# State space: B and C projected once and convolved along time by ACT and VectorE, with z and the first x tap moved forward on TensorE

## The chip, the cores and the metric

One Trainium2 chip, one NeuronCore. The metric is the device time of one execution in microseconds (us); lower is better.

## The reference

The program is a two-layer decoder over 16 sequences of 128 rows and 256 columns: in layer 0 linear attention, cross attention and a gated MLP with ternary weights, in layer 1 a state-space block, attention with 8-bit inputs and a ternary linear layer, each followed by a residual sum and a layer norm. The change touches the state-space block alone:

```python
zxbcdt = x @ W_in.T                       # z 512, xBC 768 (x 512, B 128, C 128), dt 64
z, xBC, dt_raw = ...
y = conv_general_dilated(xBC, w, padding=[(3, 0)], feature_group_count=768)   # 4 taps along time, each channel by itself
xBC = y * sigmoid(y)
dt = softplus(dt_raw + dt_bias);  a = dt * -exp(A_log)
CB = C @ B.T                              # 128 x 128 for one sequence
y = (CB * L * dt) @ x + D * x             # L[i, j] = exp(sum of a over j+1..i), lower triangle
out = rmsnorm(y * silu(z)) @ W_out.T
```

## The kernel before

All data stay in SBUF in 32-bit floats. One sequence is one tile of 128 rows. The state-space stage (`state_space`, line 1160) is a software pipeline of 18 steps m = 0 to 17, written out for each engine by `steps(m, side, attend, front, back, first)`. In step m the part called front works on sequence m + 1 (projections, convolution, softplus, decays), attend on sequence m (the seven levels of the masked product), and back on sequence m - 1 (gate, output projection, norm). Each engine runs its own fixed list, and semaphores tie the lists together. Step 0 also holds the last pieces (`tail`) of the MLP of layer 0, and steps 1 to 14 prepare the 8-bit weights of the next stage in 12 chunks: `chunk_mean` (L1585, L1587, VectorE) and `centre` (L1357, POOL) in steps 1 to 10, `chunk_high` (L1508, ACT) in steps 2 to 13, `chunk_low` (L1602, VectorE) in steps 3 to 14. GpSimd is called POOL here.

TensorE in step m, in order: dt (L1444, 2 products); B and C into the PSUM bank pC (L1451): for each half, 4 taps times 2 halves of the contraction, 16 products, whose weights are the projection's columns already multiplied by the tap's coefficient (`w_tap`), and whose moving operand is the transposed input xT shifted by the tap; levels 0 and 1 (L1404); the transposes of the gated y (L1424), which wait for VectorE's gate; z (L1462); then the eight x taps (L1410) with, before tap n = 0, 2, 4, 5, 6, levels 2 to 6; before tap 2 the product CB (L1472), which waits for `bc_in`; with tap 4 the output projection (L1433). At the end the transposes of the next input (L1392) and the seven decay sums (L1489). A product of 32-bit operands shows in the trace as two matmul records (the transposes as one).

A level waits for the VectorE product of the level two before it: `pe.wait_ge(s_term_done, level l - 2)`, since only two PSUM banks (pL) hold levels. So level 4 waits for term 2.

VectorE in step m: dt plus bias (L1296), minus |dt| (L1298), gate y (L1625), terms 0 and 1 (L1618), start of y (L1631), softplus (L1561, L1563, L1565, L1570, L1572, L1575, L1577) and a (L1580), `chunk_low`, term 2, `chunk_mean`, term 3, the masked CB (L1650, L1652), norm (L112), terms 4 and 5, residual and statistics (L1664, L98 to L103), term 6, xdt (L1671), and the scaled inputs xd of levels 0 to 3 (L1248).

ACT: exp of minus |dt| (L1524), gated y out of PSUM and its squares (L1515, L1517), Ln with its table load (L1530), Silu of B and C into bcT with its table load (L1532), Silu of z (L1534), `chunk_high`, Silu of x (L1544), the copy of the transposed input (L1286), Exp of the decays with its table load (L1548).

POOL: for each of the seven levels y += term (L1350), each waiting for its term; the root (L1338, L1340) after level 1; `centre` after levels 3 and 4; the norm's root (L107); skip (L1370); the scaled inputs of levels 4 to 6 (L1248).

The weights `w_tap` are made by `make_tap` (L1274) on VectorE in the last steps of the stage before.

Of the kernel before, what the change touches and what calls it, by code (L numbers as in the profile page):

```python
# [22 lines left out]
ACT = mybir.ActivationFunctionType  # L23
# [3 lines left out]
P = 128  # L27
# [1132 lines left out]
def state_space(nc, env, dram, ctx, spare):  # L1160
# [18 lines left out]

    w_z, w_dt, w_raw, conv_w, w_out, norm_w, dt_bias, a_neg, d_skip, spans, pairs = [env.ssm[n] for n in (  # L1180
        "z", "dt", "bcx", "conv", "out", "norm", "dt_bias", "a_log", "d", "spans", "pairs")]
    sz = sb("sz", [P, 2, HID])
# [4 lines left out]
    bcT = sb("bcT", [P, 2 * N])  # L1187
    w_tap = env.w_tap = sb("w_tap", [P, TAPS, KT, CONV])
    xT = sb("xT", [P, KT, PAD + P])
    dt_in = sb("dt_in", [P, H])  # L1190
# [23 lines left out]
             "xdt_done", "xd_vector", "cbd_done", "skip_done", "y0_done", "gated", "squared",  # L1214
             "ms_eps", "rms_done", "yT_ps", "yT_in", "o_ps")
    s = {n: sem(n, 1) for n in names}
# [55 lines left out]
    def make_tap(dve, tap):  # L1272

        last = dve.tensor_tensor(w_tap[:, tap], w_raw[:], conv_w[:, tap, :].unsqueeze(1).to_broadcast([P, KT, CONV]),  # L1274
                                 ALU.mult)
        if tap == TAPS - 1:
            last.then_inc(taps_ready, 1)
            dve.wait_ge(a_exp, 1)
            dve.tensor_scalar(a_neg[:], a_neg[:], -1.0, None, ALU.mult).then_inc(w_ready, 1)
# [107 lines left out]
    def tensor(pe, tail):  # L1387
# [7 lines left out]
        def steps(m, side, attend, front, back, first):  # L1395
# [41 lines left out]
            if front:  # L1437
                pe.wait_ge(s["xT_in"], now(m + 1, 0))
                if m > 1:
                    pe.wait_ge(norm.summed, now(m - 2, 0))  # L1440
                else:
                    pe.wait_ge(s["dec_in"], now(m, 0))
                for k in range(KT):
                    last = pe.matmul(dt_bank(m + 1), xT[:, k, PAD:PAD + P], w_dt[:, k, :],  # L1444
                                     start=(k == 0), stop=(k == KT - 1))
                last.then_inc(s["dt_ps"], 1)
                pe.wait_ge(s["cbd_done"], now(m, 0))
                for half in range(2):
                    for n in range(TAPS * KT):
                        t, k = n // KT, n % KT  # L1450
                        last = pe.matmul(pC[:, half * N:(half + 1) * N],  # L1451
                                         w_tap[:, t, k, HID + half * N:HID + (half + 1) * N],
                                         xT[:, k, t:t + P],
                                         start=(n == 0), stop=(n == TAPS * KT - 1))
                last.then_inc(s["bc_ps"], 1)
            next_level()
            next_level()
            if back:
                transpose_gated(m - 1)
            if front:  # L1460
                for k in range(KT):
# [6 lines left out]
                pe.wait_ge(s["xs_in"], now(m, 0))  # L1468
            for n in range(TAPS * KT):
                if n == 2 and front:  # L1470
                    pe.wait_ge(s["bc_in"], now(m + 1, 0))
                    pe.matmul(pC[:, 0:P], bcT[:, 0:N], bcT[:, N:2 * N], start=True, stop=True)\  # L1472
                        .then_inc(s["cb_ps"], 1)
                if n in (0, 2, 4, 5, 6):
                    next_level()
# [22 lines left out]
    def scalar(act, tail):  # L1498
# [13 lines left out]
        def steps(m, side, attend, front, back, first):  # L1512
# [7 lines left out]
            if back and not front:  # L1520
                gated_out(m - 1)
            if front:
                act.wait_ge(s["minus_abs"], now(m + 1, 0))
                act.activation(e_abs[:], e_abs[:], ACT.Exp).then_inc(s["e_done"], 1)  # L1524
# [5 lines left out]
                act.activation(log_p[:], one_p[:], ACT.Ln).then_inc(s["log_done"], 1)  # L1530
                act.wait_ge(s["bc_ps"], now(m + 1, 0))
                act.activation(bcT[:], pC[:, 0:2 * N], ACT.Silu).then_inc(s["bc_in"], 1)  # L1532
                act.wait_ge(s["z_ps"], now(m + 1, 0))
# [21 lines left out]

    def vector(dve, tail):
        def softplus(m):


            dve.wait_ge(s["e_done"], now(m, 0))  # L1560
            dve.tensor_scalar(one_p[:], e_abs[:], 1.0, None, ALU.add).then_inc(s["one_p_done"], 1)  # L1561
            dve.wait_ge(s["one_p_done"], now(m, 0))
            dve.tensor_scalar(part[:], one_p[:], -1.0, 1e-30, ALU.add, ALU.max).then_inc(s["part_min"], 1)  # L1563
            dve.wait_ge(s["part_min"], now(m, 0))
            dve.reciprocal(part[:], part[:]).then_inc(s["part_inv"], 1)  # L1565
# [689 lines left out]
def program(nc, dram, out):  # L2255
    env = Env()
    with ExitStack() as ctx:
# [31 lines left out]
        def regions(at, shapes):  # L2289
            tiles = {}  # L2290
            for n, shape in shapes:
# [5 lines left out]
                              ("out", [4, D]), ("norm", [4]), ("dt_bias", [64]), ("a_log", [64]), ("d", [64]),  # L2297
                              ("spans", [7, P]), ("pairs", [7, P])))
        with ExitStack() as xa:
# [86 lines left out]
def layouts(i):  # L2386
# [16 lines left out]
    a["ssm_win"] = t("L1_attn_W_in")  # L2403
    a["ssm_conv"] = np.broadcast_to(t("L1_attn_conv_w"), (P, 4, 768))
    a["ssm_wout"] = t("L1_attn_W_out")
    a["ssm_norm"] = np.asarray(i["L1_attn_norm_w"]).reshape(-1, P).T
# [36 lines left out]
```

## Time and profile before

| | |
|---|---|
| median of 3 runs | 2179.44 us (2178.09 to 2184.95) |
| profiled execution | 2178.37 us, span 2176.6 us |
| PE busy | 2028.2 us, 93% |
| VectorE busy | 1624.8 us, 75% |
| ACT busy | 1333.5 us, 61% |
| POOL busy | 1274.6 us, 59% |
| state-space stage | about 860 to 1274 us of the span |

The span is the profiled execution from its first to its last instruction, 1.8 us shorter than that execution's device time. Shares are means over six stages with different limits. PE is TensorE's matmuls, PEld its weight loads.

### The profile page before, as it was taken

The numbers are of one execution on the slowest core, as the hardware profiler recorded it, in microseconds if no ns is written. First come the engines' busy times: TensorE is split into PE (matmuls) and PEld (weight loads), VectorE is DVE, ScalarE is ACT, GpSimd is POOL, SyncE is SP. The second block draws the span as 40 slices with busy tenths as digits, with TensorE's granted clock in tenths as the row PEclk, the third lists the DMA queues.
The fourth block names the chain that finished last, engine by engine and source line by source line (L and its number), as shares of the span: only waits on it lengthen the run. The fifth ranks groups of instructions, "written<-read, shape, count | busy, mean of one in ns | idle before, by whom it ended". The sixth has DMA issues, their size and how long they took to land.

```text
span 2176.6 us, 35701 instructions
## 1 busy us (share of the span) xinstructions
PE 2028.2 (93%) x10116; PEld 1329.1 (61%) x10116; DVE 1624.8 (75%) x3833; ACT 1333.5 (61%) x5022; POOL 1274.6 (59%) x1550
## 2 busy tenths in 40 slices
PE   7879999999999998899999957999999999999995
PEld 5636666666666665555655524666666666666664
DVE  7845667677776777787888746788888888788886
ACT  3555666666666665333343326777777777777773
POOL 0154454455444542578876734777777777777774
PEclk9999999999999999999999979999999999999998
DMA  6000000000000003000000011000000000000000
GB/s 225 1 18 6 3 4 3 2 5 2 2 2 2 2 1 141 9 20 20 20 20 10 1 47 40 4 4 6 6 6 5 6 5 6 8 5 6 3 3 8
DMA packets 30094, 37.62 MB, mean 17 GB/s; under 512 B 3328, under 2 KB 24320, under 8 KB 29312
## 3 DMA queue, kind: packets, MB, share of 16 engines
q1 hardware_dynamic: 29952, 36.11, 5.0%
q8 instruction: 42, 0.69, 0.1%
q14 instruction: 100, 0.82, 0.1%
HBM read 34.00 MB, written 2.10 MB: 17 GB/s over the span
## 4 chain that ended last, share of the span: by engine, by line
PE 63%; DVE 15%; ACT 11%; issue 7%; POOL 3%; DMA 0%; DVEq 0%; SPq 0%; POOLq 0%; ACTq 0%
PE xa_pS L755 5%; PE xa_pJB L736 5%; PE xa_pO L830 5%; PE xa_pY L867 5%; PE fa_pJB L1910 5%; PE xa_pJA L736 4%; PE ssm_pX L1410 4%; PE fa_pS L1929 3%; PE fa_pY L1962 3%; PE fa_pO L1949 3%; PE fa_pJA L1890 2%; PE ssm_pL L1404 2%; PE fa_pH L2012 2%; PE xa_pP L747 2%; POOL fa_rs L1846 2%
## 5 line engine op out<-in xcount | busy, mean ns | idle before, releaser
L2038 ACT ACTIVATE fa_qT<-fa_pH,all_fa_head_vec 128x512 f32<-128x512 f32 x128 | 99.6, 778 | 177.9 <-PE fa_pH L2012 177.9
L1846 POOL TENSOR_TENSOR fa_rs<-fa_rs,all_minus_half 128x4 f32<-128x4 f32 x192 | 197.9, 1031 | 15.0
L1350 POOL TENSOR_TENSOR ssm_y<-ssm_y,ssm_term 128x512 f32<-128x512 f32 x112 | 142.2, 1270 | 81.5 <-DVE ssm_term L1618 57.1
L2047 ACT ACTIVATE fa_pS<-fa_pS,fa_nb 128x128 f32<-128x128 f32 x512 | 183.3, 394 | 6.0 <-issue 6.0
L1843 POOL TENSOR_TENSOR fa_rs<-fa_ms,all_eps5w 128x4 f32<-128x4 f32 x192 | 44.4, 232 | 226.8 <-ACT fa_q_junk L2031 126.4
L1929 PEld LDWEIGHTS fa_pS<-fa_kT,fa_qT 128*128 128x128 f32 x1024 | 124.1, 191 | 65.2 <-ACT fa_qT L2038 58.4
L1871 POOL TENSOR_TENSOR fa_cat<-fa_ov,fa_om 128x512 bf16<-128x512 f32 x128 | 154.0, 1203 | 5.3
L1929 PE MATMUL fa_pS<-fa_kT,fa_qT 128*128 128x128 f32 x1024 | 148.1, 288 | 2.6 <-ACT fa_qT L2038 0.9
L1862 POOL TENSOR_TENSOR fa_ov<-fa_ob,fa_om 128x512 f32<-128x512 bf16 x128 | 148.0, 1157 | 3.2 <-DVE fa_om L2225 3.2
L682 POOL TENSOR_TENSOR xa_rs<-xa_ms,all_eps 128x4 f32<-128x4 f32 (+1 forms) x65 | 13.2, 203 | 222.6 <-ACT xa_junk L906 222.6
L924 ACT ACTIVATE xa_pr<-xa_pS,xa_nb,xa_rs 128x256 f32<-128x256 f32 x256 | 142.5, 568 | 0.2
L2180 DVE TENSOR_TENSOR fa_qn<-fa_pJA,fa_rs 128x512 f32<-128x512 f32 x128 | 88.4, 690 | 69.0 <-POOL fa_rs L1846 68.9
L1962 PE MATMUL fa_pY<-all_shared_weights,fa_cat 128*128 128x256 bf16 x1024 | 133.6, 274 | 4.8 <-POOL fa_cat L1871 4.8
L2031 ACT ACTIVATE fa_q_junk<-fa_pJA 128x128 bf16<-128x128 f32 x512 | 136.4, 302 | 0.4
L2047 ACT ACTIVATION_READ_ACCUMULATOR fa_pS<-fa_pS,fa_nb 128x1 f32 x512 | 134.0, 262 | 0.0
L1890 PE MATMUL fa_pJA<-fa_w_all,fa_xq 128*128 128x512 bf16 x512 | 133.0, 383 | 0.0
L1949 PE MATMUL fa_pO<-fa_pT,fa_v 128*128 128x256 f32 x512 | 131.9, 380 | 1.1 <-DVE fa_ob L2208 1.0
L1910 PE MATMUL fa_pJB<-all_shared_weights,fa_ctxT 128*128 128x512 f32 x256 | 126.2, 617 | 5.6 <-DMA fa_ctxT<-in_ctxT 4.9
L755 PE MATMUL xa_pS<-all_shared_weights,xa_qT 128*128 128x256 f32 x512 | 126.4, 387 | 5.3 <-ACT xa_qT L931 5.2
L1410 PE MATMUL ssm_pX<-ssm_w_tap,ssm_xT 128*128 128x512 f32 x256 | 122.6, 592 | 0.0
L867 PE MATMUL xa_pY<-xa_wo,xa_oT 128*128 128x256 f32 x512 | 121.4, 380 | 1.0 <-ACT xa_oT L952 1.0
L736 PE MATMUL xa_pJA<-all_shared_weights,xa_xT 128*128 128x512 f32 x256 | 121.5, 597 | 0.4 <-DVE xa_t L987 0.2
(330 smaller groups left out, 5844.7 us busy)
## 6 DMA issues: line engine op xcount, KB each, us to landing
all_shared_weights<-in_fa_w SPq DMA_DIRECT2D x12, 512.0 KB, 3.8
fa_cat<-in_fa_wproj SPq DMA_DIRECT2D x8, 512.0 KB, 3.8
all_shared_weights<-in_xa_wq SPq DMA_DIRECT2D x1, 2048.0 KB, 13.8
xa_wo<-in_xa_wo SPq DMA_DIRECT2D x1, 2048.0 KB, 17.2
xa_ctxT<-in_ctxT SPq DMA_DIRECT2D x16, 128.0 KB, 2.1
all_shared_weights<-in_fa_wkvx SPq DMA_DIRECT2D x1, 2048.0 KB, 10.0
fa_ctxT<-in_ctxT SPq DMA_DIRECT2D x16, 128.0 KB, 2.1
out_x<-all_X SPq DMA_DIRECT2D x16, 128.0 KB, 1.7
```

Of the source, the lines that this page charges most:

```text
L736: last = pe.matmul(bank[:, :], lhs[k], w[:, k, at0:at0 + 512], start=(k == 0), stop=(k == KT - 1))
L755: last = pe.matmul(pS[b][:, (h % 2) * NK:(h % 2 + 1) * NK], qT[:, n % 2, h, :], kT[:, to, :, n, :], start=True, stop=True)
L867: last = pe.matmul(pY[:, 0:D], oT[:, h, :], w_o[:, h, :], start=(h == 0), stop=(h == G * HG - 1))
L1410: return pe.matmul(pX[:, :], xT[:, k, t:t + P], w_tap[:, t, k, 0:HID], start=(n == 0), stop=(n == TAPS * KT - 1))
L1846: pool.tensor_tensor(rs[:, j % 2, cols], rs[:, j % 2, cols], env.mhalf[:, cols], ALU.pow)\
L1871: pool.tensor_tensor(cat[:, 4 * ((j - 3) % UNITS):4 * ((j - 3) % UNITS) + 4, :], ov[:, i], om[:, i], ALU.subtract).then_inc(a["cat"], 1)
L1890: last = pe.matmul(bank[:, :], xq[:, side, st, k, :], w_all[:, part, k, cols], start=(i == 0), stop=(i == 2 * KT - 1))
L1910: last = pe.matmul(pJB[:, :], ctxT[:, side, k, :], w_kvx[:, k, c * 512:(c + 1) * 512], start=(k == 0), stop=(k == KT - 1))
L1929: last = pe.matmul(pS[n % 2][:, i * P:(i + 1) * P], qT[:, n % 2, i, :], kT[:, to, 1 if n < 4 else 0, (4 * (n % 4) + i) // 2, :], start=Tru ...
L1949: last = pe.matmul(pO[:, 2 * i * P:(2 * i + 2) * P], v[:, to, 1 if n < 4 else 0, g * HD:(g + 1) * HD], pT[:, n % 2, 2 * i:2 * i + 2, :], s ...
L1962: last = pe.matmul(pY[:, 0:D], cat[:, hd, :], w_proj[:, part, hd, :], start=(n == 0 and i == 0), stop=(n == UNITS - 1 and i == 2 * HG - 1))
L2047: last = act.activation(four(pS[j % 2])[:, i, :], four(pS[j % 2])[:, i, :], ACT.Exp, bias=nb[:, j % 2, i:i + 1], accum_out=rsum[:, j % 2, ...
```

## The change

B and C are projected once, with the plain weights and the unshifted input: 4 products in place of 32/2 = 16. The result in pC has channels on partitions and time along the free dimension. ACT multiplies each half by the coefficient of the last tap (one for each partition) and puts it into `bc_sum`, a piece of `w_tap` that is no longer read; VectorE adds the three shifted taps of each half in six instructions, between `one_p` and the rest of softplus; ACT's Silu then reads `bc_sum`. On TensorE, z and x tap 0 now stand right behind B and C, ahead of levels 0 and 1; taps 1 to 7 follow, levels 2 to 6 stand before taps 2 to 6, and CB stands before tap 4. `make_tap` multiplies 512 columns in place of 768, and the first one also copies the 256 columns of B and C. One small load of 4 KB is added.

```diff
+    bc_sum = w_tap[:, 1, 0, HID:CONV]
...
+    SHIFTS = ((1, 0), (1, 1), (2, 0), (2, 1), (3, 0), (3, 1))
+    bc_added = sem("bc_added", len(SHIFTS))
...
     def make_tap(dve, tap):
-        last = dve.tensor_tensor(w_tap[:, tap], w_raw[:], conv_w[:, tap, :].unsqueeze(1).to_broadcast([P, KT, CONV]),
-                                 ALU.mult)
+        if tap == 0:
+            dve.tensor_copy(w_tap[:, 0, :, HID:CONV], w_raw[:, :, HID:CONV])
+        last = dve.tensor_tensor(w_tap[:, tap, :, 0:HID], w_raw[:, :, 0:HID],
+                                 conv_w[:, tap, 0:HID].unsqueeze(1).to_broadcast([P, KT, HID]), ALU.mult)
...
                 for half in range(2):
-                    for n in range(TAPS * KT):
-                        t, k = n // KT, n % KT
+                    for k in range(KT):
                         last = pe.matmul(pC[:, half * N:(half + 1) * N],
-                                         w_tap[:, t, k, HID + half * N:HID + (half + 1) * N],
-                                         xT[:, k, t:t + P],
-                                         start=(n == 0), stop=(n == TAPS * KT - 1))
+                                         w_tap[:, 0, k, HID + half * N:HID + (half + 1) * N],
+                                         xT[:, k, PAD:PAD + P], start=(k == 0), stop=(k == KT - 1))
                 last.then_inc(s["bc_ps"], 1)
-            next_level()
-            next_level()
-            if back:
-                transpose_gated(m - 1)
-            if front:
                 for k in range(KT):
                     last = pe.matmul(pZ[:, :], xT[:, k, PAD:PAD + P], w_z[:, k, :],
                                      start=(k == 0), stop=(k == KT - 1))
...
                 pe.wait_ge(s["xs_in"], now(m, 0))
-            for n in range(TAPS * KT):
-                if n == 2 and front:
+                tap(0)
+            next_level()
+            next_level()
+            if back:
+                transpose_gated(m - 1)
+            for n in range(1, TAPS * KT):
+                if n == 4 and front:
                     pe.wait_ge(s["bc_in"], now(m + 1, 0))
                     pe.matmul(pC[:, 0:P], bcT[:, 0:N], bcT[:, N:2 * N], start=True, stop=True)\
                         .then_inc(s["cb_ps"], 1)
-                if n in (0, 2, 4, 5, 6):
+                if 2 <= n < LEVELS:
                     next_level()
...
             if front:
+                act.wait_ge(s["bc_ps"], now(m + 1, 0))
+                for half in range(2):
+                    last = act.activation(bc_sum[:, half * N:(half + 1) * N], pC[:, half * N:(half + 1) * N], ACT.Copy,
+                                          scale=conv_bc[:, 4 * half + PAD:4 * half + PAD + 1])
+                last.then_inc(s["bc_scaled"], 1)
                 act.wait_ge(s["minus_abs"], now(m + 1, 0))
...
-                act.wait_ge(s["bc_ps"], now(m + 1, 0))
-                act.activation(bcT[:], pC[:, 0:2 * N], ACT.Silu).then_inc(s["bc_in"], 1)
+                act.wait_ge(bc_added, now(m + 1, 0, len(SHIFTS), len(SHIFTS) - 1))
+                act.activation(bcT[:], bc_sum, ACT.Silu).then_inc(s["bc_in"], 1)
...
+        def convolve_bc(m):
+            dve.wait_ge(s["bc_scaled"], now(m, 0))
+            for j, (shift, half) in enumerate(SHIFTS):
+                if j >= 2:
+                    dve.wait_ge(bc_added, now(m, 0, len(SHIFTS), j - 2))
+                to = bc_sum[:, half * N + shift:(half + 1) * N]
+                at = 4 * half + PAD - shift
+                dve.scalar_tensor_tensor(out=to, in0=pC[:, half * N:(half + 1) * N - shift],
+                                         scalar=conv_bc[:, at:at + 1], in1=to, op0=ALU.mult, op1=ALU.add)\
+                    .then_inc(bc_added, 1)
+
         def softplus(m):
             dve.wait_ge(s["e_done"], now(m, 0))
             dve.tensor_scalar(one_p[:], e_abs[:], 1.0, None, ALU.add).then_inc(s["one_p_done"], 1)
+            convolve_bc(m)
             dve.wait_ge(s["one_p_done"], now(m, 0))
```

## Rows read from the trace of the kernel before

**Rows 1.** Busy us over nine steps: PE, PEld, DVE, ACT, POOL; clock, DMA share, GB/s

```profile
960.54:1174.29 213.75, 209.44 (x902) 127.67 (x901) 174.26 (x302) 81.68 (x135) 169.06 (x141) 1.00 0.08 23
```

**Rows 2.** Timeline, TensorE in one step (start, length, engine, line, count, idle before)

```profile
1081.26 3.79 PE L1451 MATMUL ssm_pC<-ssm_xT,ssm_w_tap 128*128 128x128 f32 x32
1084.89 1.88 PE L1404 MATMUL ssm_pL<-ssm_xd,ssm_cb 128*128 128x512 f32 x4
1086.98 0.66 PE L1424 MATMUL ssm_pY<-all_ident,ssm_y 128*128 128x128 f32 x4 [0.21 <-DVE ssm_y L1625]
1092.20 0.49 PE L1472 MATMUL ssm_pC<-ssm_bcT 128*128 128x128 f32 x2 [0.27 <-ACT ssm_bcT L1532]
1095.10 1.02 PE L1404 MATMUL ssm_pL<-ssm_xd,ssm_cb 128*128 128x512 f32 x2
```

**Rows 3.** Timeline, VectorE and POOL from the start of y to term 2, same step

```profile
1088.71 0.18 DVE L1561 TENSOR_SCALAR ssm_one_p<-ssm_e_abs 128x64 f32<-128x64 f32 x1
1088.87 2.61 POOL L1350 TENSOR_TENSOR ssm_y<-ssm_y,ssm_term 128x512 f32<-128x512 f32 x2 [1.00 <-DVE ssm_y L1631]
1088.93 1.26 DVE L1563 TENSOR_SCALAR ssm_part<-ssm_one_p 128x64 f32<-128x64 f32 x1
1090.22 0.55 DVE L1565 RECIPROCAL ssm_part<-ssm_part 128x64 f32<-128x64 f32 x1
1090.81 0.75 DVE L1570 TENSOR_TENSOR ssm_part<-ssm_part,ssm_log_p 128x64 f32<-128x64 f32 x1
...
1092.51 1.41 DVE L1602 SCALAR_TENSOR_TENSOR fa_w_all<-all_shared_weights,all_fa_in_scale,fa_w_all 128x512 bf16<-128x512 f32 x2
1093.84 0.68 DVE L1618 TENSOR_TENSOR ssm_term<-ssm_pL,ssm_dec 128x512 f32<-128x512 f32 x1
```

**Rows 4.** Timeline, VectorE and POOL across the step's end

```profile
1101.21 2.60 POOL L1350 TENSOR_TENSOR ssm_y<-ssm_y,ssm_term 128x512 f32<-128x512 f32 x2
...
1103.67 0.69 DVE L1671 TENSOR_TENSOR ssm_xdt<-ssm_xs,ssm_dt 128x512 f32<-128x512 f32 x1 [1.43 <-ACT ssm_xs L1544]
1103.77 1.00 POOL L107 TENSOR_TENSOR ssm_rstd<-ssm_mean_var,all_minus_half 128x1 f32<-128x1 f32 x1
...
1104.74 1.07 POOL L1370 TENSOR_TENSOR ssm_skip<-ssm_xs,all_shared_weights 128x512 f32<-128x512 f32 x1
...
1105.87 2.29 DVE L1248 TENSOR_TENSOR ssm_xd<-ssm_xdt,ssm_dec 128x2048 f32<-128x2048 f32 x1 [1.51 <-ACT ssm_dec L1548]
```

**Rows 5.** VectorE and ACT forms that bound the new instructions (ns min/median/max)

```profile
L1664 DVE SCALAR_TENSOR_TENSOR ssm_res<-ssm_pO,ssm_rms,all_X x16: 469/475/484, 934.0 to 1274.1; 128x256 f32<-128x256 f32 x16
L1652 DVE SCALAR_TENSOR_TENSOR ssm_junk<-ssm_pC,all_ident x16: 273/276/281, 881.3 to 1240.5; 128x128 f32<-128x128 f32 x16
L1563 DVE TENSOR_SCALAR ssm_part<-ssm_one_p x16: 195/1255/1257, 870.1 to 1234.3; 128x64 f32<-128x64 f32 x16
L2047 ACT ACTIVATE fa_pS<-fa_pS,fa_nb x512: 331/396/434, 1329.4 to 2143.7; 128x128 f32<-128x128 f32 x171
```

**Rows 6.** ACT, timeline of the same step: its wait before L1524

```profile
1085.46 0.26 ACT L1524 ACTIVATE ssm_e_abs<-ssm_e_abs 128x64 f32<-128x64 f32 x1 [3.44 <-DVE ssm_e_abs L1298]
```

**Rows 7.** Timeline of step 0, where the MLP's tail runs

```profile
869.97 0.62 PE L784 MATMUL xa_pJB<-all_ident,mlp_hq 128*128 128x128 bf16 x8 [1.23 <-DVE mlp_hq L1031]
...
872.59 0.28 PE L888 MATMUL xa_pO<-all_ident,mlp_xq 128*128 128x128 bf16 x2
```

**Rows 8.** The four instructions that make the taps (ns min/median/max)

```profile
L1274 DVE TENSOR_TENSOR ssm_w_tap<-all_shared_weights x4: 1750/1750/1751, 839.7 to 856.8; 128x1536 f32<-128x1536 f32 x4
```

**Rows 9.** TensorE after a long and after a shorter wait, timeline

```profile
1253.33 3.59 PE L1404 MATMUL ssm_pL<-ssm_xd,ssm_cb 128*128 128x512 f32 x4 [3.48 <-issue]
...
1212.88 0.49 PE L1472 MATMUL ssm_pC<-ssm_bcT 128*128 128x128 f32 x2 [2.19 <-ACT ssm_bcT L1532]
```

**Rows 10.** Granted clock around these two waits (windows, columns as in Rows 1)

```profile
1254.00:1256.00 2.00, 2.00 (x3) 0.67 (x2) 1.29 (x2) 0.00 (x0) 2.00 (x3) 0.50 0.00 0
...
1213.00:1216.00 3.00, 2.94 (x8) 1.16 (x8) 2.86 (x8) 0.32 (x1) 1.13 (x3) 1.00 0.00 0
```

More of the change, by code:

```diff
@@ L1177, in state_space @@
     sb, ps, sem = sp_.sb, sp_.ps, sp_.sem
-    w_z, w_dt, w_raw, conv_w, w_out, norm_w, dt_bias, a_neg, d_skip, spans, pairs = [env.ssm[n] for n in (
-        "z", "dt", "bcx", "conv", "out", "norm", "dt_bias", "a_log", "d", "spans", "pairs")]
+    w_z, w_dt, w_raw, conv_w, w_out, norm_w, dt_bias, a_neg, d_skip, spans, pairs, conv_bc = [
+        env.ssm[n] for n in (
+            "z", "dt", "bcx", "conv", "out", "norm", "dt_bias", "a_log", "d", "spans", "pairs", "conv_bc")]
     sz = sb("sz", [P, 2, HID])
@@ L1214, in state_space @@
              "xdt_done", "xd_vector", "cbd_done", "skip_done", "y0_done", "gated", "squared",
-             "ms_eps", "rms_done", "yT_ps", "yT_in", "o_ps")
+             "ms_eps", "rms_done", "yT_ps", "yT_in", "o_ps", "bc_scaled")
+    SHIFTS = ((1, 0), (1, 1), (2, 0), (2, 1), (3, 0), (3, 1))
+    bc_added = sem("bc_added", len(SHIFTS))
     s = {n: sem(n, 1) for n in names}
@@ L2297, in program @@
                               ("out", [4, D]), ("norm", [4]), ("dt_bias", [64]), ("a_log", [64]), ("d", [64]),
-                              ("spans", [7, P]), ("pairs", [7, P])))
+                              ("spans", [7, P]), ("pairs", [7, P]), ("conv_bc", [8])))
         with ExitStack() as xa:
@@ L2404, in layouts @@
     a["ssm_conv"] = np.broadcast_to(t("L1_attn_conv_w"), (P, 4, 768))
+    a["ssm_conv_bc"] = np.asarray(i["L1_attn_conv_w"])[512:].reshape(2, P, 4).transpose(1, 0, 2).reshape(P, 8)
     a["ssm_wout"] = t("L1_attn_W_out")
```

## The prediction

> **What bounds the kernel now.** I read the busy time by window first, then one step of the state-space stage engine by engine. Nine steps take 213.75 us, so a step is 23.75 us [rows 1]. TensorE is busy for 209.44 of them, at the full clock of 2.4 GHz (granted 1.00), which looks like a bound; VectorE has 174.26 and POOL 169.06. The timeline corrects this. TensorE stops twice in a step, before the transposes of the gated y and before CB, for 0.21 and 0.27 us [rows 2]. But level 4 must wait for term 2, and term 2 ends at 1093.84 + 0.68 = 1094.52, level 4 starts at 1095.10 [rows 2, 3]: VectorE runs only 0.58 us ahead. And at the step's end POOL's last two additions end at 1103.81 and VectorE's xdt starts at 1103.67, as soon as the last one lets it [rows 4]. So three engines are bound within some tenths of a us of each other, and taking work off one of them pays only until the next one holds.
>
> The second thing to see is how VectorE and POOL hold each other up. L1563 handles 64 columns and takes 1.26 us, from just after POOL's first addition starts until that addition is over; alone it takes 0.195 (minimum, rows 5). L1570 does the same behind the second one [rows 3]. Each addition lasts 1.3 us and holds both off for some 1.15 of it. L1664, with one operand in PSUM, has 469 to 484 ns in 16 of 16, whatever POOL does [rows 5].
>
> **TensorE: what goes.** 32 records of B and C take 3.79 us, less the 0.16 by which a record outlasts the next one's start (1084.89 - 1081.26 = 3.63) [rows 2]. 8 remain, 0.91 us; 2.72 us go in each of 16 steps, 43.5 us in all. In their place, ahead of level 0, come z (four records of 512 columns like those of the two levels, 1.72 us, 1.88 less 0.16) and tap 0 (0.86): 2.58 us. Levels 0 and 1 thus start where they did, about when xd is done. The transposes wait for the gate as before. After them come taps 1 to 3 and levels 2 and 3, 5 x 0.86 = 4.3 us: from 1086.98 + 0.5 to 1091.78. CB still stands at 1092.20, since bcT comes from ACT's chain of two table loads, which starts at `one_p` and does not move (the new VectorE work that it also needs is done 1.7 us before, below). CB ends at 1092.53, and level 4 waits for term 2, until now 1094.52. So the 2.72 us saved turn into a wait of about 2.6 us before level 4, if nothing else changes.
>
> **VectorE: what comes.** Six additions of 125 to 128 columns, one operand in PSUM, with a coefficient for each partition. No row has this form at this width. Upper bound: L1664, the same form at 256 columns, 0.475 us. Lower bound: L1652, 128 columns but no coefficient, 0.276 us. A column costs about 1.05 ns (0.68 us for 512 columns in term 2, 2.29 for 2,048 in xd) [rows 3, 4], so I take 0.475 - 0.13 = 0.34 us, from the row with the same form. VectorE starts the next instruction about 0.08 us before the last one's record ends (1092.51 + 1.41 against 1093.84) [rows 3], so six take 5 x 0.265 + 0.34 = 1.67 us. They start at 1088.71 + 0.11 = 1088.82, and L1563 comes to the queue at about 1090.4. That is the point that decides. Before, it waited for POOL's first addition only; now the second one is already running, and it gets through with that, where L1570 gets through now, at 1091.56 - 0.23 = 1091.33. Then 0.20, the reciprocal 0.55 and L1570 0.23 with their gaps end at 1092.36, in place of 1091.56: **0.80 us later**, not 1.67, since half of the new work lies where VectorE stood waiting anyway. Term 2 ends at 1095.32, level 4 starts at 1095.37 in place of 1095.10: +0.27.
>
> POOL's later additions all hang on the terms, so its last one ends 0.80 later too, which is 0.53 later against TensorE. Then xdt, which now starts at once, waits 0.53; POOL's root and skip come behind it, and skip holds off xd (1105.87) by about 0.38 [rows 4]. I add it: a step costs 0.27 + 0.38 = **0.65 us more**, where POOL also has its `centre` work and its shadow (steps 3 to 11), and 0.27 where not (12 to 14).
>
> **ACT.** Two copies of 128 columns with a coefficient: 0.40 us is the row with one such operand [rows 5], bounds 0.33 and 0.43; together 0.8. They stand where ACT idles 3.44 us for minus |dt| [rows 6], right after B and C, which are now done 2.7 us earlier, at about 1082.3. Cost 0; if that cover were gone, 0.8 a step.
>
> **The edges.** In step 15 there is no `chunk_low` (1.41 us), so term 2 is no longer last and TensorE keeps some of its gain: 1.41 - 0.27 = about -1.1. The same in steps 1 and 2, where the pipeline fills; -1.5 together, less sure. In step 0 the 1.67 us come ahead of the MLP's tail on VectorE, whose input leads to TensorE's transposes at 872.59 with about 0.3 to spare: +1.3; and the shorter B and C earn nothing there, because TensorE waits 1.23 us for VectorE right after [rows 7]. The four instructions that make the taps fall from 1.75 us for 1,536 columns to 1,024: -0.53 each, and the first gets a copy of 512 columns, between 0.2 (L1563 alone) and 0.53; they mostly lie beside TensorE work, I take -0.3 [rows 8], bounds 0 and -1.8. One more load, of 4 KB, ahead of the taps: 0, since L1274 is one instruction in a list that goes on with the stage before; no row bounds it.
>
> **Sum**, against the profiled execution's 2178.37: 9 x 0.65 = 5.9, 3 x 0.27 = 0.8, step 15 -1.1, steps 1 and 2 -1.5, step 0 +1.3, taps -0.3: +5.1 us, **2183.5 us**. The median of the three runs is 2179.44, 1.1 above the profiled one; against it this is +0.2%. About 0.3%, 6.5 us, is what a measurement of this kernel can tell from no change.
>
> **The rivals.**
> (a) *The new additions are short enough for L1563 to slip in between POOL's two additions.* If they take 0.276 each (lower bound), they end at 1090.05, and L1563 asks just as the first addition lets go, as it does now. Then VectorE is not delayed at all; level 4 gains up to 0.53 and POOL's end gives back 0.38 of it: -0.15 in nine steps, -0.5 in three, -1.9 in step 15, -2.2 in steps 1 and 2, +1.0 in step 0, taps -0.3: -6.3, about 2172. The Trainium skill, VectorE: DVE Perf Modes, section "The TRN2 errata", gives 120 cycles plus the columns at 0.96 GHz for an operand in PSUM, 0.26 us here, and by that figure this case would hold; L1664, by the same formula 0.39 us, measures 0.475 [rows 5], so the trace disagrees. Chance 0.13.
> (b) *TensorE is the bound after all*, and its gain shows: the slack that I give VectorE's chain is larger than the rows say. 16 x 2.72 = 43.5 less, 2135. Against it: term 2 ends only 0.58 us before level 4. Chance 0.05.
> (c) *The clock falls in the new wait.* TensorE would stand from 1091.78 to 1095.4 with only CB (0.33 us) in it. After a wait of 3.48 us the two levels behind it took 3.59 us in place of 1.88, and the clock was 0.50 (1.2 GHz); after one of 2.19 us it stayed at 1.00 [rows 9, 10]. The new wait, about 2.9 after CB, lies between. It decides from the point where the chip takes CB for idleness; each fall costs 1.7 us on the chain that sets the step. In all twelve steps it is 20 us more, 2204; in a third of them 2190. This is the case on the other side. Chance 0.15.
> (d) *POOL holds the six additions off too.* Then the first waits for POOL's first addition and the second for the next: softplus ends 1.9 us late, 15 x 1.9 = 28, about 2212. L1664's steadiness speaks against it. The Trainium skill, SBUF — State Buffer, section "Who interferes with whom", says that an instruction with at most one input in SBUF does not contend with GpSimd; by that rule too this case is out. Chance 0.05.
> That B and C cost less on TensorE than before is certain from the code; a change that does nothing is not a case here.
>
> **How the numbers follow.** The forecast has 0.62; its own spread, from additions of 0.30 to 0.475 us (the upper bound puts L1563 behind the second addition, +0.3 a step) and from the edges, is 2179 to 2188. The range 2170 to 2195 takes in all of that, (a) and the milder half of (c); outside are (b), (d) and the worse half of (c). Faster by over 0.3%: (b), a good half of (a) and a little of the forecast's edge, 0.17. Slower: (d), most of (c) and the upper end of the forecast, 0.29. Within: 0.54.
>
> **What would show it.** Right: TensorE's busy time in the same nine steps falls by about 24 us while the step grows to about 24.4; L1404's idle time names term L1618 with 2.5 to 3 us before level 4 in each step; L1563 still lasts about 0.9 us and L1570 drops to 0.23; the six additions last 0.34 each; xd starts behind skip, not behind the decays. Wrong: a step of 23.6 with L1563 at 0.2 is (a); a step near 21 is (b); a granted clock under 1.00 in the middle of the stage is (c); additions over 0.5 us are (d).

## The result and the profile after

The changed kernel takes 2207.09 us (median of 4 runs, 2206.32 to 2208.28), against 2180.11 us for the kernel before on the same chip (4 runs, 2178.09 to 2184.95). The ratio is 1.0124, with a 95% interval of 1.0112 to 1.0136: slower by 1.2%. The prediction was 2183.5 with a range of 2170 to 2195, so the result lies outside it, on the slow side.

First the clock and the busy shares in 40 slices, from the page of the kernel after:

```profile
span 2205.8 us, 35052 instructions
...
PE 2017.8 (91%) x9732; PEld 1305.4 (59%) x9732; DVE 1638.0 (74%) x3930; ACT 1342.1 (61%) x5054; POOL 1269.4 (58%) x1550
...
PEclk9999999999999999998989878999999999999998
```

A slice is 55 us, and a 9 stands for 90% or more of the full clock. Slices 19, 21 and 23, inside the state-space stage, are now at 8; the dip at and behind its end (slices 24 and 25) is in the kernel before too, with a 7 in slice 24. The windows of the stage show it without the other stages (columns as in [rows 1]; the first row is of the kernel before, the second of the kernel after):

```profile
940.00:1200.00 260.00, 254.73 (x1091) 154.79 (x1091) 213.86 (x371) 99.07 (x164) 203.89 (x170) 1.00 0.06 19
```

```profile
940.00:1200.00 260.00, 225.95 (x742) 125.34 (x742) 201.08 (x392) 95.82 (x168) 182.86 (x155) 0.91 0.06 19
```

TensorE is busy for 28.8 us less in the same 260 us and yet the stage takes longer; the granted clock has a mean of 0.91 in place of 1.00. From here on step m is measured from the start of ACT's xs for sequence m to that for m + 1. The nine steps of [rows 1] are steps 4 to 12, 23.75 us each. In the kernel after they are 26.05, 27.23, 27.26, 25.60, 25.89, 27.15, 27.23, 27.26 and 25.60: a mean of 26.59, and not constant. Step 3, ahead of them, takes 24.30 us.

**A step in which the clock holds** (step 3, kernel after; the timeline of TensorE, then of VectorE, then of POOL, answering to [rows 2, 3]):

```profile
941.43 1.88 PE L1461 MATMUL ssm_pZ<-all_shared_weights,ssm_xT 128*128 128x512 f32 x4
943.15 1.02 PE L1416 MATMUL ssm_pX<-ssm_w_tap,ssm_xT 128*128 128x512 f32 x2
944.01 1.88 PE L1410 MATMUL ssm_pL<-ssm_xd,ssm_cb 128*128 128x512 f32 x4
...
951.55 0.49 PE L1476 MATMUL ssm_pC<-ssm_bcT 128*128 128x128 f32 x2 [0.30 <-ACT ssm_bcT L1541]
954.80 1.10 PE L1410 MATMUL ssm_pL<-ssm_xd,ssm_cb 128*128 128x512 f32 x2 [2.76 <-DVE ssm_term L1639]
955.73 1.89 PE L1439 MATMUL ssm_pO<-all_shared_weights,ssm_yT 128*128 128x256 f32 x8
957.46 1.02 PE L1416 MATMUL ssm_pX<-ssm_w_tap,ssm_xT 128*128 128x512 f32 x2
```

```profile
948.03 0.18 DVE L1581 TENSOR_SCALAR ssm_one_p<-ssm_e_abs 128x64 f32<-128x64 f32 x1
948.13 1.62 DVE L1573 SCALAR_TENSOR_TENSOR ssm_w_tap<-ssm_pC,all_shared_weights,ssm_w_tap 128x127 f32<-128x127 f32 x6
949.67 1.17 DVE L1584 TENSOR_SCALAR ssm_part<-ssm_one_p 128x64 f32<-128x64 f32 x1
950.88 0.55 DVE L1586 RECIPROCAL ssm_part<-ssm_part 128x64 f32<-128x64 f32 x1
951.46 0.22 DVE L1591 TENSOR_TENSOR ssm_part<-ssm_part,ssm_log_p 128x64 f32<-128x64 f32 x1
...
953.97 0.68 DVE L1639 TENSOR_TENSOR ssm_term<-ssm_pL,ssm_dec 128x512 f32<-128x512 f32 x1
```

```profile
948.18 2.61 POOL L1356 TENSOR_TENSOR ssm_y<-ssm_y,ssm_term 128x512 f32<-128x512 f32 x2 [1.00 <-DVE ssm_y L1652]
```

This is the step that the prediction described: z and tap 0 ahead of level 0, six additions in 1.62 us, L1584 done behind POOL's second addition and L1591 then at its full speed, and level 4 waiting 2.76 us for term 2 (L1639; [rows 3] has it as L1618).

**A step in which the clock falls** (step 6; kernel after, timeline of TensorE):

```profile
1029.03 0.49 PE L1476 MATMUL ssm_pC<-ssm_bcT 128*128 128x128 f32 x2 [0.30 <-ACT ssm_bcT L1541]
1032.28 2.04 PE L1410 MATMUL ssm_pL<-ssm_xd,ssm_cb 128*128 128x512 f32 x2 [2.77 <-DVE ssm_term L1639]
1034.12 3.62 PE L1439 MATMUL ssm_pO<-all_shared_weights,ssm_yT 128*128 128x256 f32 x8
1037.53 1.49 PE L1416 MATMUL ssm_pX<-ssm_w_tap,ssm_xT 128*128 128x512 f32 x2
1038.86 1.02 PE L1410 MATMUL ssm_pL<-ssm_xd,ssm_cb 128*128 128x512 f32 x2
```

and its windows (the granted clock is the third number from the end):

```profile
1030.00:1031.00 1.00, 0.00 (x0) 0.00 (x0) 1.00 (x3) 0.68 (x2) 0.00 (x0) 1.00 0.00 0
1031.00:1032.00 1.00, 0.00 (x0) 0.00 (x0) 1.00 (x2) 0.00 (x0) 0.00 (x0) 0.82 0.00 0
1032.00:1033.00 1.00, 0.72 (x1) 0.50 (x2) 1.00 (x2) 0.00 (x0) 0.72 (x1) 0.50 0.46 55
...
1037.00:1038.00 1.00, 1.00 (x3) 0.69 (x3) 0.00 (x0) 0.00 (x0) 1.00 (x2) 0.50 0.00 0
1038.00:1039.00 1.00, 1.00 (x3) 0.38 (x2) 0.00 (x0) 0.00 (x0) 0.83 (x1) 0.76 0.00 0
```

The wait is the same, but inside it, at about 1031.6, the clock goes from 2.4 to 1.2 GHz and stays there until about 1038.5. Level 4 takes 2.04 us in place of 1.10, the output projection 3.62 in place of 1.89, the next tap 1.49 in place of 1.02: 3.1 us, and the step is 27.26. In the steps of 25.6 to 26.05 us the clock is down for half as long, 3.4 us (1058.9 to 1062.4 in step 7; two of its windows):

```profile
1058.00:1059.00 1.00, 0.00 (x0) 0.00 (x0) 1.00 (x3) 0.00 (x0) 0.00 (x0) 0.97 0.00 0
...
1062.00:1063.00 1.00, 1.00 (x6) 0.83 (x5) 1.00 (x5) 0.00 (x0) 1.00 (x2) 0.82 0.02 8
```

In steps 7 and 12 (25.60) it falls at the same point of the wait, and level 4 (2.05 in step 7) and a part of the output projection (2.38) are slowed; in steps 4 and 8 (26.05 and 25.89) it falls behind level 4, and the output projection (3.27 in step 4) and the tap (1.38) are slowed.

**Where the 29.2 us went** (span 2205.8 against 2176.6). The stage's first xs starts 2.0 us later (885.35 against 883.32); steps 1 to 3 take 77.46 us against 77.22; steps 4 to 12 take 25.5 more; steps 13 to 15 take 80.90 against 74.09, 6.8 more; and 5.4 us come back behind the last xs.

### The profile page after: what moved, and what is told of

Same layout as the page of the kernel before. It is cut to its first block, busy times and chain, and to the rows that moved or that the text cites. A ratio compares the mean times of both kernels' runs of the same rounds, so it can differ in the third digit from the quotient of the medians.

```text
span 2205.8 us, 35052 instructions
## 1 busy us (share of the span) xinstructions
PE 2017.8 (91%) x9732; PEld 1305.4 (59%) x9732; DVE 1638.0 (74%) x3930; ACT 1342.1 (61%) x5054; POOL 1269.4 (58%) x1550
## 4 chain that ended last, share of the span: by engine, by line
PE 65%; DVE 17%; ACT 8%; issue 6%; POOL 3%; DMA 0%; SPq 0%; POOLq 0%; ACTq 0%; DVEq 0%
PE xa_pJB L736 5%; PE fa_pJB L1931 5%; PE xa_pS L755 5%; PE xa_pO L830 5%; PE xa_pY L867 5%; PE fa_pS L1950 4%; PE xa_pJA L736 4%; PE fa_pY L1983 3%; PE fa_pO L1970 3%; PE fa_pJA L1911 3%; PE ssm_pX L1416 3%; PE fa_pH L2033 3%; PE ssm_pL L1410 2%; PE ssm_pO L1439 2%; PE fa_pJB L1911 2%
## 5 line engine op out<-in xcount | busy, mean ns | idle before, releaser
L1410 PE MATMUL ssm_pL<-ssm_xd,ssm_cb 128*128 128x512 f32 x224 | 123.0, 646 | 45.6 <-DVE ssm_term L1639 42.1
L1416 PE MATMUL ssm_pX<-ssm_w_tap,ssm_xT 128*128 128x512 f32 x256 | 132.6, 614 | 0.0
```

The costliest lines, as they stand in the source:

```text
L1410: pe.matmul(pL[in_turn(side, l)][:, :], cb[:, side, l, :], xd[:, side, l, :], start=True, stop=True).then_inc(level_ps, 1)
L1416: return pe.matmul(pX[:, :], xT[:, k, t:t + P], w_tap[:, t, k, 0:HID], start=(n == 0), stop=(n == TAPS * KT - 1))
```

## The experiments

Theory A: the chain VectorE, POOL, level 4 costs what the prediction says (about 0.65 us a step), and everything above it is the clock, which falls because TensorE now stands for 2.8 us before level 4. Rival B: VectorE's or POOL's chain is longer than foreseen, and the clock falls only as a consequence. Rival C: it is the new place of z and tap 0. All times are compared with the kernel before on the same chip (medians 2179.97 to 2180.87).

**1. The wait filled with spare work.** Twelve products ahead of CB, into a part of PSUM that nothing reads:

```diff
                     pe.wait_ge(s["bc_in"], now(m + 1, 0))
+                    for f in range(12):
+                        pe.matmul(pC[:, 2 * N:3 * N], w_tap[:, 0, f % KT, HID:HID + N], xT[:, f % KT, PAD:PAD + P],
+                                  start=(f == 0), stop=(f == 12 - 1))
```

> Twelve spare products of B's weights (24 records, about 2.7 us) stand on TensorE between the wait for bc_in and CB, into unused columns of pC; nothing else differs from the changed kernel. Theory A (the clock falls in the wait before level 4, and TensorE then works at 1.2 GHz through level 4, the output projection and tap 4): the wait shrinks to about 0.3 us, the granted clock stays 1.00 through steps 2 to 14, every step takes about 24.4 us, the kernel about 2183 us. Theory B (the longer step is VectorE's and POOL's chain, the clock only goes along): the step stays near 26.5 us and the kernel near 2207, or above it by the spare work.

Measured: 2186.76 us, ratio 1.0031 (1.0020 to 1.0042). Adding TensorE work takes 20.3 us off the changed kernel. The windows of the stage, and one step of its timeline:

```profile
940.00:1200.00 260.00, 251.14 (x1078) 152.18 (x1077) 219.92 (x422) 107.05 (x187) 198.73 (x166) 1.00 0.06 19
```

```profile
1051.57 2.94 PE L1477 MATMUL ssm_pC<-ssm_xT,ssm_w_tap 128*128 128x128 f32 x24 [0.30 <-ACT ssm_bcT L1544]
1054.36 0.39 PE L1479 MATMUL ssm_pC<-ssm_bcT 128*128 128x128 f32 x2
1054.83 1.10 PE L1410 MATMUL ssm_pL<-ssm_xd,ssm_cb 128*128 128x512 f32 x2
1055.76 1.89 PE L1439 MATMUL ssm_pO<-all_shared_weights,ssm_yT 128*128 128x256 f32 x8
```

The clock is 1.00, and steps 4 to 12 have a mean of 24.35 us (eight of them 24.35 to 24.37), which is +0.60 over the 23.75 of [rows 1]. So the mean of 26.59 in the changed kernel is 0.60 of chain and 2.24 of clock. Theory A holds, though its time was 3.8 us too low; B does not hold, since VectorE and POOL do exactly the same work here.

**2. Less filling.** The same with 4 products, 0.9 us of work:

```diff
-                    for f in range(12):
+                    for f in range(4):
```

> The changed kernel with 4 spare products (about 0.9 us of TensorE's work) in the wait, where the run with 12 (2.7 us) gave 2186.8 and the run with none 2207.1. If what counts is that the wait is filled at all, the clock holds and it is about 2187; if what counts is how much idle time is left (here some 1.9 us, where waits of 1.9 and 2.1 us in the runs without adds and with the old order lost the clock in some steps), about a third of the steps fall and it is 2190 to 2196; if each step needs nearly all of the filling, it stays at 2203 to 2207.

Measured: 2186.89 us, ratio 1.0030 (1.0018 to 1.0043), the same as with 12. A wait of 1.87 us stays, and two of the nine steps (26.04 and 26.06) still lose the clock; the other seven take 24.20 to 24.36. A third of the filling does nearly all of it. That the two runs come out alike has a second reason: in steps 2 and 15 the wait is shorter than 12 products, which lengthen these steps (24.73 and 23.88 us in run 1, 22.89 and 22.88 here). The expectation for "how much idle time is left" (2190 to 2196) was too high, and "filled at all" too simple.

**3. z and tap 0 back in their old place,** the single projection and its convolution kept:

```diff
-                (z and tap(0)) ... next_level(); next_level(); transpose_gated(m - 1)
+                next_level(); next_level(); transpose_gated(m - 1) ... (z and tap(0))
```

> B and C projected once and convolved on their channels, but z and tap 0 back in their old places. Theory A: the 2.7 us that TensorE saves turn into a wait before level 0 (about 2.2 us, for xd), which is short enough for the clock to stay at 1.00; level 4 waits little; a step is 24.2 to 24.4 us, the kernel 2180 to 2186 us. Theory B: the same VectorE work, so the same step as in the changed kernel, near 26.5 us, 2207 us.

Measured: 2184.87 us, ratio 1.0019 (1.0007 to 1.0031). TensorE now stands before level 0, for xd, and the clock falls there too (timeline of steps 8 and 11; four records of a level at full clock end in 1.88 us):

```profile
1066.69 2.82 PE L1410 MATMUL ssm_pL<-ssm_xd,ssm_cb 128*128 128x512 f32 x4 [2.14 <-issue]
...
1140.74 1.95 PE L1410 MATMUL ssm_pL<-ssm_xd,ssm_cb 128*128 128x512 f32 x4 [2.29 <-issue]
```

In step 8 the clock falls behind a wait of 2.14 us, in step 11 it holds behind one of 2.29. The mean clock from 940 to 1200 is 0.95 where the expectation had 1.00, but the step is 24.54 us, hardly more than in run 1. The saved time now stands as a wait early in the step, and slow work behind it eats the slack that TensorE has before term 2; in the changed kernel the slow work lies behind the last wait that the step has to spare. A mean of 0.95 is also some 26 us at half clock in these 260, against 47 at 0.91, so a part of the gain is that the clock is down for less long. So C is half right: with the old order the clock falls as well, but it costs little.

**4. The six additions left out:**

```diff
-            convolve_bc(m)
...
-                act.wait_ge(bc_added, now(m + 1, 0, len(SHIFTS), len(SHIFTS) - 1))
```

> The six VectorE additions are left out (B and C get only their last tap, so the output differs), all else as in the changed kernel. My account of VectorE's delay: L1584 waits for POOL's first addition only and term 2 ends 0.8 us earlier against one_p, so the wait before level 4 is about 2.0 us in place of 2.77. If the clock then holds, a step is 23.4 to 23.6 us and the kernel about 2168 us. If the clock falls all the same, about 2190 us. Theory B: 1.7 us less per step, 2180 us, with the clock as low as now.

Measured: 2181.99 us, ratio 1.0004 (0.9994 to 1.0015). The wait before level 4 is 1.94 to 1.95 us and the clock falls in 4 of the 11 steps that have it (3 to 13); those take 25.1 to 25.2 us, the others 23.4 to 23.5. TensorE's timeline, three consecutive steps:

```profile
1003.62 1.10 PE L1410 MATMUL ssm_pL<-ssm_xd,ssm_cb 128*128 128x512 f32 x2 [1.94 <-DVE ssm_term L1637]
...
1027.15 1.10 PE L1410 MATMUL ssm_pL<-ssm_xd,ssm_cb 128*128 128x512 f32 x2 [1.95 <-DVE ssm_term L1637]
...
1050.69 2.05 PE L1410 MATMUL ssm_pL<-ssm_xd,ssm_cb 128*128 128x512 f32 x2 [1.95 <-DVE ssm_term L1637]
```

The same work, the same wait: twice the clock holds, and once level 4 takes 2.05 us. The additions cost 24.35 - 23.5 = 0.85 us a step, what the prediction gave their delay on VectorE (0.80). Even with no additions at all the change would bring only 0.2 us in a step (23.75 - 23.5), and the 2168 us expected for a held clock was too low: the next run gives 2178.

**5. The same, filled** with 8 products, 1.8 us:

```diff
-            convolve_bc(m)
...
+                    for f in range(8):
+                        pe.matmul(pC[:, 2 * N:3 * N], ...)
```

> The changed kernel without VectorE's six adds (left out: the convolution of B and C past the first tap) and with 8 spare products of B's weights, about 1.8 us of TensorE's work, in the wait ahead of C by B. Theory A: the step is 23.4 us in all of 940:1200 with the clock at 1.00, as in the four fifths of the steps of the run without the adds in which the clock held, and the kernel is 2176 to 2180, less than the run with neither (2182). Rival (the steps of 25.1 there came of something else than the clock, or the spare products lengthen the step): 2182 or more.

Measured: 2177.97 us, ratio 0.9992 (0.9982 to 1.0002). Eight steps of 23.53 to 23.55 and one of 23.39, clock 1.00. So the steps of 25.1 were the clock, and in these steps the spare products cost nothing (in steps 2 and 15, where the wait is shorter, they cost 1.0 and 0.9 us against run 4).

**6. Term 2 earlier on VectorE,** behind the reciprocal, where the rest of the softplus and the chunk's low part no longer lie ahead of it (the six additions still do):

```diff
             if front:
                 softplus(m + 1)
+            terms(2)
...
             chunk_low(m - 3)
-            terms(2)
             chunk_mean(m - 1)
```

> The changed kernel with term 2 moved on VectorE from behind chunk_low to behind the reciprocal of softplus. Theory A: term 2 ends about 2.6 us earlier, level 4 follows CB at once, the clock stays 1.00; then the step is set by term 3, POOL and the decays: 22 to 23.5 us, the kernel 2150 to 2170 us. Theory B: the chain of VectorE is as long as before, 2200 us or more.

Measured: 2184.57 us, ratio 1.0013 (1.0003 to 1.0023). The one wait of 2.77 us becomes two. Timeline of TensorE:

```profile
1051.88 1.10 PE L1410 MATMUL ssm_pL<-ssm_xd,ssm_cb 128*128 128x512 f32 x2 [0.75 <-DVE ssm_term L1639]
...
1057.40 1.10 PE L1410 MATMUL ssm_pL<-ssm_xd,ssm_cb 128*128 128x512 f32 x2 [1.84 <-DVE ssm_term L1639]
```

The clock holds (1.00), but seven steps take 24.72 or 24.73, and the time is between what A and B expected: term 3 still stands behind the chunk's low part and mean (2.8 us) and is now what is late. This takes off 22.5 us without one instruction more or less.

**7. Term 3 earlier too,** behind the softplus's end:

```diff
                 softplus_end(m + 1)
+            terms(3)
...
             chunk_mean(m - 1)
-            terms(3)
```

> On the changed kernel, VectorE computes term 2 behind the reciprocal and term 3 behind the softplus's end, both ahead of the chunk's mean and low parts. Theory A (the saved TensorE time is lost at the waits for terms 2 and 3, and at the clock that falls in them): with both terms ahead of the work that can wait, level 4's wait goes to about 0.8 us, level 5's from 1.85 to under 0.6, the clock stays 1.00 in 940:1200, the step is 23.0 to 23.6 and the kernel 2165 to 2175, faster than both. Rival (VectorE's or POOL's chain of adds sets the step, wherever the terms stand): the step stays at 24.7 and the kernel at 2184.

Measured: 2208.46 us, ratio 1.0126 (1.0109 to 1.0143): a miss, all of run 6's gain is gone. The timelines of VectorE and POOL show why, and TensorE's what follows:

```profile
1039.64 2.41 DVE L1623 SCALAR_TENSOR_TENSOR fa_w_all<-all_shared_weights,all_fa_in_scale,fa_w_all 128x512 bf16<-128x512 f32 x2
1041.97 1.21 DVE L1606 TENSOR_REDUCE all_shared_weights<-all_shared_weights 128x8 f32<-128x1024 f32 x1
```

```profile
1039.87 1.64 POOL L1356 TENSOR_TENSOR ssm_y<-ssm_y,ssm_term 128x512 f32<-128x512 f32 x1 [1.60 <-DVE ssm_term L1639]
```

```profile
1045.66 1.89 PE L1410 MATMUL ssm_pL<-ssm_xd,ssm_cb 128*128 128x512 f32 x2 [3.27 <-DVE ssm_term L1639]
1047.34 2.83 PE L1416 MATMUL ssm_pX<-ssm_w_tap,ssm_xT 128*128 128x512 f32 x4
```

Term 3 releases POOL's addition, and the chunk's low part, with both operands in SBUF, now runs beside it: its two instructions take 2.41 us where they took 1.41 [rows 3], and the addition 1.64 where it took 1.3. Behind it come the reduction, cb and term 4, so that level 6 waits 3.27 us for term 4, and the clock falls there: 1.89 us in place of 1.10, and 2.83 for four records in place of 1.88. The late term only moved. Steps 5 and 10, in which the clock does not fall, still take 25.03 us.

**8. Its control:** the same two terms moved in the kernel before.

> The control: the same two terms moved to the same places in the kernel before, which keeps both projections. Theory A: TensorE is busy 98% of its step there, so at most the 0.3 to 0.4 us a step in which it is not can go: 2176 to 2181. Rival (the order on VectorE is worth the same whatever TensorE does): as much less than the kernel before as the moved terms take off the changed one with its clock held, 10 us or more, near 2170.

Measured: 2185.29 us, ratio 1.0026 (1.0016 to 1.0036); steps 4 to 12 have a mean of 24.19 us. Neither theory said slower. The low part is held up in the same way (2.41 us in its timeline), level 6 waits 0.34 us for term 4, and a step is 0.4 us longer.

**9. The chunk's mean in VectorE's idle time.** Term 2 as in run 6; the mean (1.21 + 0.17 us) leaves the row ahead of term 3 and goes, one chunk earlier, between the product xs by dt and the wait for the decays, 1.51 us in [rows 4]:

```diff
             chunk_low(m - 3)
-            terms(2)
-            chunk_mean(m - 1)
             terms(3)
...
                     .then_inc(s["xdt_done"], 1)
+            chunk_mean(m)
+            if front:
                 dve.wait_ge(s["xdt_done"], now(m + 1, 0))
```

> The changed kernel with term 2 behind the reciprocal, and the chunk's mean (1.21 + 0.17 us of VectorE in every step, ahead of term 3) taken out of the row and put, for the next chunk, between the product xs by dt and the wait for the decays, where VectorE waits 1.51 us. Theory A, from the run with term 2 early (24.73 us a step, waits of 0.75 and 1.84 us before levels 4 and 5): the second wait goes to about 0.5 us, the clock stays at 1.00, the step is 23.2 to 23.6 and the kernel 2166 to 2172, faster than both. Rival (POOL's chain of adds, or the mean running beside POOL's skip product, holds the inputs of the next step by as much): 24.4 to 24.8 a step and 2181 to 2185.

Measured: 2178.74 us, ratio 0.9988 (0.9978 to 0.9998). Of steps 4 to 12 seven are as forecast, 23.38 to 23.40, one is 22.87, and one takes 30.60, for which this line of the waits stands:

```profile
DVE all_shared_weights L1606 <- DMA all_shared_weights<-in_fa_w: 7.2, 1, 7.2
```

SyncE starts the fourth chunk's transfer only at 962.93, after it has waited 93.1 us for the stage's first normalised output (`norm.x_done`; the waits of SyncE below). It lands at 966.56, and the mean, taken one step sooner, has to wait for it.

```profile
SPq L67 <- DVE all_X L112: 93.1, 1, 93.1
```

**10. The control of run 9:** both moves in the kernel before.

> The control: both moves on the kernel before, with its two projections. Theory A: TensorE has 21.3 + 2.7 = 24.0 us of work and short waits in its step there and is the bound, so nothing is to be had: 23.7 to 24.3 a step, 2178 to 2185. Rival (the moves themselves are what pays, whichever way B and C are made): 2166 to 2172 here too.

Measured: 2189.81 us, ratio 1.0033 (1.0021 to 1.0045). Seven steps take 23.74 or 23.75 as they did, one 24.72, and one 30.14 with the same transfer. The moves by themselves bring nothing there: TensorE's work fills the step. The kernel as a whole is 10 us slower than the kernel before: the one step costs 6.4 us, and in the profiled execution the first xs comes 4.8 us later (888.16 against 883.32).

**11. Run 9, with the fourth chunk's mean left where it was:**

```diff
+            if m == RAWS + 1:
+                chunk_mean(RAWS)
             terms(3)
...
-            chunk_mean(m)
+            if m != RAWS:
+                chunk_mean(m)
```

> The run with the late mean, but the fourth chunk's mean goes back to its old place in the step after, since there VectorE waited 7.15 us once for that chunk's transfer and the step took 30.60 us where the others took 23.39. Theory A: the 7.2 us go, all else stays, 23.4 us a step, 2170.5 to 2173 where the run with the late mean gave 2178.7: ratio to the kernel before 0.994 to 0.997, faster than both. Rival (what the transfer held up comes back elsewhere, in the last stage's first weights): 2176 to 2180.

Measured: 2170.45 us, ratio 0.9956 (0.9943 to 0.9970). This is faster than the kernel before by 0.4% and than the changed one by 1.7%. Against the kernel before, the steady steps give only a part of it. By the profiles the span is 8.2 us shorter: steps 1 to 3 give 3.0 us, steps 4 to 12 2.4, steps 13 to 15 2.0 and the rest of the span behind the last xs 3.3, less the 2.4 us by which the first xs comes later. The same edit on the kernel before was not run; run 10's undisturbed steps stand in for it. Waits of TensorE over 962 to 1202 (us in total, times, longest), and the stage's window:

```profile
PE ssm_pL L1410 <- DVE ssm_term L1639: 14.6, 28, 1.9
PE ssm_pY L1430 <- DVE ssm_y L1646: 3.5, 10, 0.5
PE ssm_pC L1476 <- ACT ssm_bcT L1541: 3.0, 10, 0.3
```

```profile
940.00:1200.00 260.00, 235.80 (x840) 125.95 (x839) 237.94 (x436) 107.45 (x189) 205.77 (x172) 1.00 0.06 19
```

**12. Beside it, term 3 ahead of the chunk's low part.**

> As the run beside it, with term 3 ahead of the chunk's low part (1.41 us of VectorE) instead of behind it. Level 5's wait was 0.52 us and goes; level 6's term 4 comes out no sooner, since the same VectorE work lies ahead of it. If level 5's wait is part of the step, 23.0 to 23.2 a step and 2167 to 2170; if VectorE's row as a whole sets the step (22.1 us of work in 23.39), the step stays at 23.4 and the kernel at 2171 to 2173.

Measured: 2184.96 us, ratio 1.0021 (1.0012 to 1.0030), a miss by both expectations. As in run 7 the low part runs beside POOL's addition, and term 4, which level 6 waits for, is late. Timelines of VectorE and TensorE:

```profile
1029.92 2.41 DVE L1623 SCALAR_TENSOR_TENSOR fa_w_all<-all_shared_weights,all_fa_in_scale,fa_w_all 128x512 bf16<-128x512 f32 x2
```

```profile
1034.62 1.10 PE L1410 MATMUL ssm_pL<-ssm_xd,ssm_cb 128*128 128x512 f32 x2 [1.94 <-DVE ssm_term L1639]
```

The order of two neighbours in VectorE's row decides 14.5 us: most steps take 24.36 us in place of 23.40, and the clock falls in steps 4, 8 and 13. I had twice counted VectorE's work by its length and not by what runs on POOL beside it.

The runs side by side (mean of steps 4 to 12, from the starts of xs; the longest wait of a level for a term, as it recurs in the steps):

```
                              us       step    longest wait     clock 940:1200
before                        2180     23.75   none             1.00
after                         2207.1   26.59   2.77 (level 4)   0.91
1  12 spare products          2186.8   24.35   filled           1.00
2  4 spare products           2186.9   24.68   1.87 (level 4)   0.99
3  old place of z, tap 0      2184.9   24.54   none; 2.14 xd    0.95
4  no additions               2182.0   24.01   1.94 (level 4)   0.97
5  no additions, 8 products   2178.0   23.52   0.2              1.00
6  term 2 early               2184.6   24.37   1.84 (level 5)   1.00
7  terms 2 and 3 early        2208.5   26.32   3.27 (level 6)   0.93
8  before, with 7's moves     2185.3   24.19   0.34 (level 6)   1.00
9  term 2 early, mean late    2178.7   24.13   0.75 (level 4)   0.99
10 before, with 9's moves     2189.8   24.57   none             0.99
11 as 9, one mean left        2170.5   23.49   0.75 (level 4)   1.00
12 as 11, term 3 first        2185.0   24.68   1.94 (level 6)   0.99
```

The means of runs 9 and 10 hold the one step of 30 us.

## Why the prediction was wrong

The step that failed is **rival (c), its chance and its price**. The prediction named the mechanism, the place, and even the time: "in all twelve steps it is 20 us more, 2204". It then gave it 0.15. The two rows that it had, a fall after 3.48 us and none after 2.19 us [rows 9, 10], have the new wait between them, near their middle, and nothing in the profile spoke for 0.15 rather than 0.5. The sum of 2183.5 therefore has no term for the clock, on no evidence, and the range left out the worse half of (c). Measured against run 1, the clock costs 2.24 us a step in steps 4 to 12. One row without a fall could not bound it: in run 4 waits of 1.95 us with the same work around them stand both with a fall and without.

The price was also short. 1.7 us a fall came from two levels at half clock [rows 9]. Measured against run 1, step by step, eleven steps (4 to 14) lose 1.2 to 2.9 us and step 15 0.7, 25.4 us together. Where the clock falls in the wait and is down for about 7 us, level 4, the output projection and a tap are slow, all on the path that sets the step, and it costs 2.8 to 2.9 us; where it is down for 3.4 us, 1.2 to 1.7. Had (c) been the forecast, 2204 would have been 3 us off; its price per fall was too low by a quarter.

Point by point:
- **TensorE saves 2.72 us a step and it becomes a wait of 2.6 to 2.9 before level 4.** Right: 2.76 and 2.77, and the busy time in 260 us falls by 28.8 (slower records included).
- **Six additions: 0.34 each, 1.67 together.** Right: 328 to 345 ns over 96, 1.62 together. The Trainium skill, VectorE: DVE Perf Modes, section "The TRN2 errata", gives for 128 columns an estimate of 0.26 us by its formula; measured is 0.33, and the measurement decides. The additions have one operand in SBUF and the other in PSUM, and beside POOL's additions (948.18 to 950.79 in step 3) they take no longer than elsewhere, as SBUF — State Buffer, section "Who interferes with whom", in the same skill says. So (a) and (d) are out.
- **VectorE +0.80.** Right: against [rows 3] the product with the logarithm (L1591 for L1570) ends 0.90 later in step 3, 0.10 of which was there before the six additions; without the additions the step is 0.85 shorter (run 4 against run 1). L1584 takes 1.17 us, where 0.9 was forecast.
- **Level 4 +0.27, skip and xd +0.38, together 0.65.** The sum is right (0.60 in run 1), but by luck, since the split is not: level 4 is 0.5 later in its step and the step's end gives only some 0.1 more. xd is 2.45 us long in run 1 in place of 2.29 [rows 4], not held until skip is over.
- **Edges.** Steps 1 and 2: -0.3 (forecast -1.5); step 2 gives 1.7, but step 1 takes 1.4 more, with a wait of 3.31 us before a level and one more fall of the clock. Steps 12 and 13: +0.46 and +0.51 in run 1 (forecast +0.27). Step 15: 22.88 us in run 2, -0.87 (forecast -1.1); in the changed kernel the clock took it. Step 0 lies ahead of the first xs, which comes 2.0 us later (forecast +1.3 and -0.3 for the taps); but it differs by more among kernels that differ little up to there (881.89 in run 8, 888.16 in run 10), so this shows nothing. ACT's two copies take 0.62 us together, behind C and ahead of a wait, and cost nothing, as said.
- **Not foreseen:** behind the last xs the changed kernel is 5.4 us shorter. It is not this run alone: in all profiles with the additions the rest of the span is 922.8 to 926.1 us, in all without them (the kernel before, runs 4, 5, 8, 10) 928.0 to 928.8. In that stage the weight loads' wait for the normalised queries falls from 24.1 to 17.8 us (24.1 in run 4, 17.6 in run 11). What the additions have to do with it was not tried and stays open.
- **(b), TensorE as the bound**, is out in its plain form. But run 11 shows that part of it is to be had: a step of 23.4 with 2 us of waits still in it.

## What to carry to other kernels

Work taken off the busiest engine of a loop in which others are nearly as busy can turn into a wait, as here, and a wait of TensorE has a price of its own: ask where the saved time will stand, what runs right behind it, and whether that is on the path. If the rows at hand leave it open whether the clock holds, let both cases carry the forecast. To get something out of such a change, the order on the engine that is late next has to be made anew, and there an instruction counts by what runs beside it.

## What was not expected of the hardware

- A wait of 2.77 us before level 4, with CB (0.49 us) and another wait of 0.30 us ahead of it, took the clock to 1.2 GHz in ten steps in a row (4 to 13); one of 2.76 us in step 3 did not. In step 6 it stayed there for about 7 us (1031.6 to 1038.5), through 6 us of unbroken work; in step 7, after the same wait, for 3.4 us.
- The length of the wait doesn't decide alone: at 1.94 to 1.95 us, with the same work around it, the clock fell in 4 of 11 steps (run 4), at 1.87 us in 2 of 11 (run 2), at 1.84 us, a second wait of 0.75 us ahead of it, in none of 8 (steps 3 to 10 of run 6). In run 3 it fell behind 2.14 us and held behind 2.29. What decides between like waits stays open.
- 0.9 us of useless products in the wait, a third of it, save 20 us (run 2). Moving one term forward saves 22.5 us with no instruction more (run 6), and with the chunk's mean moved too it is 36.6 (run 11).
